# Two attention blocks with experts on one core: routers read raw rows, TensorE adds a residual, GpSimd a bias, and half of the second first-layer weights moves

## The reference

```
x = x + cross_attention_0(layernorm(x), ctx)     # 16 heads of 8, rotary, distance bias, gate
x = x + experts_0(layernorm(x))                  # 8 experts, top 2, 128 -> 512 -> 128, biases
x = x + cross_attention_1(layernorm(x), ctx)     # 16 heads of 8, biases, output W_O and b_O
x = x + experts_1(layernorm(x))                  # top 2 of 8, at most 321 pairs an expert, + its input
```

## Time and profile before

| | us |
|---|---|
| median of three executions | 300.12 |
| the profiled execution | 298.92 |
| its span in the profile | 297.2 |
| busy: TensorE / its weight loads | 219.6 / 178.3 |
| busy: VectorE / ScalarE / GpSimd | 154.0 / 113.4 / 143.8 |
| TensorE busy between 25 and 50, of 25 | 23.22 |
| TensorE busy between 75 and 90, of 15 | 6.38 |
| TensorE busy between 255 and 270, of 15 | 15.00 |

### The profile page before, as it was taken

How to read it: one execution, slowest core, us unless ns; L and a number is a source line. 1 busy time by engine, 2 the same in 40 slices (tenths; PEclk the granted TensorE clock), 3 DMA queues, 4 the chain that set the end, 5 groups by cost and what they waited for, 6 DMA issues and landing times.

```text
span 297.2 us, 4760 instructions
## 1 busy us (share of the span) xinstructions
PE 219.6 (74%) x1616; PEld 178.3 (60%) x1616; DVE 154.0 (52%) x509; ACT 113.4 (38%) x212; POOL 143.8 (48%) x201
## 2 busy tenths in 40 slices
PE   1779999998434589999904878998858069999900
PEld 1657776665323469999903666555445049999900
DVE  3985567766755524343204866587475313343206
ACT  1434667664020324444513248867300204433200
POOL 5652299433566414565645460320656713565730
PEclk9999999999555569999985999999555659999985
DMA  7999993000011270010157700000100153001125
GB/s 226 305 205 350 305 215 101 0 2 10 28 37 36 63 188 21 16 30 14 39 197 231 314 1 0 0 2 2 37 18 30 39 132 104 21 29 35 34 61 160
DMA packets 26960, 27.04 MB, mean 91 GB/s; under 512 B 3208, under 2 KB 23987, under 8 KB 26677
## 3 DMA queue, kind: packets, MB, share of 16 engines
q1 hardware_dynamic: 23776, 21.56, 26.5%
q0 software_dynamic: 2560, 4.08, 4.2%
q10 hardware_dynamic: 597, 1.06, 1.1%
HBM read 16.82 MB, written 10.79 MB: 93 GB/s over the span
## 4 chain that ended last, share of the span: by engine, by line
PE 51%; DVE 17%; DMA 9%; issue 7%; ACT 7%; POOL 7%; POOLq 1%; SPq 0%; DVEq 0%
PE ps L1491 14%; PE ps L1234 6%; ACT probT L681 5%; PE ps L1480 4%; PE ps L1481 4%; PE ps L1483 4%; POOL sent L532 3%; PE ps L1260 3%; DMA back<-probT,pairu 3%; DMA xe<-sent 2%; DVE stats L821 2%; PE ps L1240 2%; PE ps L1386 2%; DMA xe<-back 2%; PE ps L1206 2%
## 5 line engine op out<-in xcount | busy, mean ns | idle before, releaser
L579 POOL DMA_INDIRECT back<-probT,pairu x48 | 46.5, 968 | 31.8 <-issue 11.8
L1491 PE MATMUL ps<-w,hT 128*128 128x128 f32 (+1 forms) x384 | 49.5, 274 | 0.0
L1491 PEld LDWEIGHTS ps<-w,hT 128*128 128x128 f32 (+1 forms) x384 | 47.6, 182 | 0.1
L1186 PE MATMUL ps<-blank,identr 128*128 128x256 f32 x74 | 27.6, 533 | 22.4 <-DMA sent<-hidk,slotu 11.7
L532 POOL DMA_INDIRECT sent<-hidk,slotu x32 | 31.9, 996 | 22.0 <-DVE slotu L936 13.5
L681 ACT ACTIVATE probT<-ps 77x1024 f32<-77x1024 f32 x32 | 32.6, 1020 | 20.4 <-PE ps L1240 13.5
L1186 PEld LDWEIGHTS ps<-blank,identr 128*128 128x128 f32 x74 | 19.1, 273 | 26.8 <-issue 12.5
L842 DVE TENSOR_REDUCE peak<-ps 128x8 fp32r<-128x616 f32 x32 | 25.3, 792 | 17.2 <-PE ps L1206 16.9
L547 POOL TENSOR_TENSOR w1lo<-hT,w1hi 128x256 fp32r<-128x256 f32 x32 | 23.6, 742 | 18.5 <-ACT w1hi L659 16.7
L716 ACT ACTIVATE hT<-ps,col 128x384 f32<-128x384 f32 x32 | 18.1, 580 | 26.5 <-PE ps L1483 26.5
L1234 PE MATMUL ps<-qst,kst 100*78 100x256 f32 x128 | 25.0, 297 | 3.6 <-ACT probT L681 3.4
(11 more groups left out here) (165 smaller groups left out, 424.0 us busy)
## 6 DMA issues: line engine op xcount, KB each, us to landing
sent<-blank SPq DMA_DIRECT2D x16, 193.5 KB, 7.6
xe<-sent SPq DMA_DIRECT2D x16, 193.5 KB, 4.2
back<-blank SPq DMA_DIRECT2D x16, 128.0 KB, 4.5
hT<-w1b SPq DMA_DIRECT2D x4, 512.0 KB, 5.1
w<-w2b SPq DMA_DIRECT2D x1, 2048.0 KB, 13.3
hT<-w1d SPq DMA_DIRECT2D x4, 512.0 KB, 5.8
xe<-back SPq DMA_DIRECT2D x8, 256.0 KB, 3.6
w<-w2d SPq DMA_DIRECT2D x1, 2048.0 KB, 9.5
```

What stands on the lines that cost most here:

```text
L579: pool.indirect_dma_start(back[m], bass.IndirectOffsetOnAxis(ap=pairu[0:n, e, c:c + 1], axis=0), ye[0:n, e, c, :], None, bounds_check=NPAI ...
L1186: pe.matmul(ps[:, bank, 0:GQ], ident, blank[:, 0:2, 0:D], start=True, stop=True)
L1491: last = pe.matmul(ps[0:n, 6 + k % 2, c * P:(c + 1) * P], hT[:, e % 2, f, c * P:c * P + n], w2[:, e, f, :], start=(f == 0), stop=(f == FC ...
```

## The change

The routers' weights are centred once (TensorE multiplies them by the identity less 1/128), so that logits come from the rows themselves; the factor of the layernorm is put on the logits in `choose` (block 0) or on the difference of the two best (block 1). `turn` therefore transposes `xres`. In block 0 `lead` writes the gate's bias and, by a product with the identity, the residual into PSUM ahead of `project`, and `projected` goes. In block 1 GpSimd adds the output bias to the rows (`shifted`), and `residual` is one addition. Two pieces of the second first-layer weights go to `hid` and `hidb`, loaded when the experts have begun; the other two are loaded behind the gather. All steps get new places, now fractions of turns and one for each group; `due` sorts by them, and a turn of TensorE and ScalarE has several points at which steps are taken.

```diff
-WARM_TAIL = [{}, {20: 2, 21: 1, 23: 2, 24: 1}]
...
+PE_STEPS = [dict(lead=(7.73, 9.2, 13.8, 17.9),
+                 project=(7.83, 11.3, 15.73, 18.47),
+                 turn=(11.5, 15.76, 18.97, 19),
+                 logits=(12.86, 17.6, 19, 19.2),
+                 ranks=(14.64, 17.7, 19.03, 19.4),
+                 next_context=(14.2,),
+                 next_parts=(19.63,),
+                 next_keys=(19.66,)),
+            dict(project=(7.44, 12.97, 18.07, 18.13),
+                 turn=(9.4, 14.8, 18.31, 18.31),
+                 logits=(10.41, 16, 18.34, 18.34),
+                 ranks=(14.38, 18.1, 18.44, 19.33))]
+DVE_STEPS = [dict(taken=(7.5, 11.8, 15.27, 16.6),
+                 attended=(8.53, 12.33, 15.3, 17.1),
+                 residual=(10.07, 14.57, 17.6, 18.3),
+                 stats=(11.1, 14.7, 17.63, 18.7),
+                 hidden=(13.1, 15.9, 18.87, 20.03),
+                 choose=(14.7, 17.6, 18.83, 19.2),
+                 slots=(16.6, 17.8, 18.84, 19.4),
+                 next_context=(18.06,),
+                 next_parts=(20.63,),
+                 next_keys=(20.7,)),
+            dict(taken=(7.76, 11.6, 14.77, 17.1),
+                 attended=(9.34, 12.6, 15.3, 17.2),
+                 residual=(9.43, 14.57, 17.13, 17.6),
+                 stats=(10.2, 14.6, 17.17, 18.13),
+                 hidden=(10.63, 15.5, 20.43, 21),
+                 choose=(14.1, 17, 17.73, 20.53),
+                 slots=(15, 17.43, 19.9, 21))]
+ACT_STEPS = [dict(tanh=(8.47, 12.13, 17.4, 17.54),
+                 copies=(11.8, 17.13, 20.67, 20.7),
+                 turned=(12.43, 17, 17.57, 17.9),
+                 high=(0.17, 0.47, 3.56, 7.5, 7.93, 8.47, 10.94, 13.28)),
+            dict(copies=(14.44, 16.03, 19.22, 19.72),
+                 turned=(10.38, 15.01, 17.16, 18.19),
+                 high=(-1, -0.97, -0.94, -0.67, -0.64, 0.03, 6.66, 7.7))]
+POOL_STEPS = [dict(deviation=(18.07, 18.1, 19.87, 19.93),
+                 send=(18.1, 19.9, 19.93, 20.47),
+                 low=(3.22, 3.73, 3.76, 20.57)),
+            dict(deviation=(11.43, 11.43, 18.67, 19.1),
+                 shifted=(0, 0, 1.96, 2.09),
+                 residual=(11.46, 21, 21, 21),
+                 send=(16, 19.03, 20.16, 20.43),
+                 low=(-2, -1, 0.03, 4.59))]
...
+def due(steps, first, last):
+
+    return [(name, GROUPS - len(places) + g if len(places) < GROUPS else g)
+            for at, name, g, places in sorted((at, name, g, places) for name, places in steps.items()
+                                              for g, at in enumerate(places)) if first <= at < last]
...
+        early = [t[:].rearrange("p t d -> p (t d)").rearrange("p (e f) -> p e f", f=FF) for t in (hid, hidb)]
+
+        def first_raw(m, k):
+
+            if m == 0:
+                return raw[:, k % RAWS]
+            return early[k] if k < len(early) else raw[:, k - len(early)]
...
-                    sp.wait_ge(s_down[0], SC * E)
-                    sp.wait_ge(s_past, 1)
-                    for k in range(RAWS):
+                    sp.wait_ge(s_xres[0], GROUPS)
+                    sp.wait_ge(s_xT[0], PIECE)
+                    for k in range(len(early)):
                         first_weights(1, k)
...
+                    sp.wait_ge(s_past, 1)
+                    for k in range(len(early), PIECES):
+                        first_weights(1, k)
                     sp.dma_start(w2[:], w2d.rearrange("p (e c d) -> p e c d", e=E, c=FC)).then_inc(s_w2[1], 16)
-                    for k in range(RAWS, PIECES):
-                        first_weights(1, k)
...
+            def shifted(g):
+
+                pool.wait_ge(s_sum[0], GT * (g + 1))
+                bo = row[:, R_BO:R_BO + D].unsqueeze(1).broadcast_to([P, GT, D])
+                pool.tensor_tensor(base[:, of_group(g), :], xres[:, of_group(g), :], bo, ALU.add).then_inc(s_xb, 1)
...
-            low_weights(1, 0)
+            for name, k in due(POOL_STEPS[1], -9, 0):
+                low_weights(1, k)
             for g in range(GROUPS):
                 deviations(of_group(g))
...
+                if m == 1 and e == 0:
+                    act.wait_ge(s_past, 1)
...
 
                     dve.wait_ge(s_tanh, g + 1)
+                    if g == 0:
+                        dve.wait_ge(s_hbase, 2 * B)
+                    dve.scalar_tensor_tensor(out=ytok[:, s, :], in0=norm[:, s, :], scalar=1.0,
+                                             in1=ps[:, BY, :].rearrange("p (t n d) -> p t n d", t=GT, n=2)[:, :, 0],
+                                             op0=ALU.add, op1=ALU.mult).then_inc(s_yread, 1)
                     dve.wait_ge(s_yread, g + 1)
...
+                    dve.wait_ge(s_xb, g + 1)
+                    dve.tensor_tensor(xres[:, s, :], ps[:, BY, 0:GQ].rearrange("p (t d) -> p t d", t=GT), base[:, s, :],
+                                      ALU.add).then_inc(s_xres[1], 1)
+
+            def stats_of(m, g):
+
+                dve.wait_ge(s_xres[m], g + 1)
+                variances(xres[:, rows_of(g), :], GT, GT * g)
...
+                deviation = 1 + 2 * B + (GROUPS * 2 * m) + g + 1
                 if m == 0:
-                    bg = gbias[:].unsqueeze(1).broadcast_to([P, GT, E])
-                    link(dve.scalar_tensor_tensor(out=logit[:, s, :], in0=lp, scalar=GATE_DIV, in1=bg,
-                                                  op0=ALU.mult, op1=ALU.add))
-                else:
-                    link(dve.tensor_copy(logit[:, s, :], lp))
-                for t in range(GT * g, GT * g + GT):
-                    last = dve.max(top[:, t, :], logit[:, t, :])
+                    dve.wait_ge(s_rstd, deviation)
+                    for k in range(GT):
+                        t = GT * g + k
+                        last = dve.scalar_tensor_tensor(out=logit[:, t, :], in0=lp[:, k, :], scalar=rstd[:, t:t + 1],
+                                                        in1=gbias[:], op0=ALU.mult, op1=ALU.add)
...
+                if m == 1:
+                    dve.wait_ge(s_rstd, deviation)
+                    dve.tensor_tensor(wdif[:, s], wdif[:, s], rstd[:, s], ALU.mult).then_inc(s_dif[1], 1)
...
+            def lead(a, g):
+
+                if g == 0:
+                    pe.wait_ge(s_gate, 1)
+                    pe.wait_ge(s_hbase, 2 * B)
+                else:
+                    pe.wait_ge(s_yread, g)
+                    pe.wait_ge(s_tanh, g)
+                for k in range(GT):
+                    pe.matmul(ps[:, BY, k * GQ:(k + 1) * GQ], gateo, gater, start=(k == 0), stop=False,
+                              skip_group_check=True)
+                    pe.matmul(ps[:, BY, k * GQ:k * GQ + D], ident, hidb[:, GT * g + k, :], start=False, stop=False,
...
-                pe.wait_ge(s_hid[m], g + 1)
+                pe.wait_ge(s_xres[m], g + 1)
...
-                transposed(route_bank(g), lambda k: hidk[:, GT * g + k, 0, 0:D], GT).then_inc(s_hTp[m], 1)
+                transposed(route_bank(g), lambda k: xres[:, GT * g + k, :], GT).then_inc(s_hTp[m], 1)
...
+                    pe.wait_ge(s_slot[0], GROUPS)
+                    pe.wait_ge(s_most, 1)
...
+                pe.wait_ge(s_iset, 9)
+                pe.matmul(ps[:, BR, 2 * D:2 * D + 2 * E], centre, router[:].rearrange("p m e -> p (m e)"),
+                          start=True, stop=True)
...
+                    turn_steps(u, u + 0.2)
                     if u < UNITS:
                         shifted_scores(a, u)
+                    turn_steps(u + 0.2, u + 0.4)
                     query_steps(a, u + 2)
                     if u + 2 < UNITS:
                         maxima(a, u + 2)
                     if u + 3 < UNITS:
                         scores(a, u + 3)
+                    turn_steps(u + 0.4, u + 0.6)
                     if AHEAD <= u < UNITS + AHEAD:
                         attend(a, u - AHEAD)
-                    if u >= UNITS + AHEAD:
-                        warm_up(WARM_TAIL[a].get(u, 0), 1)
-                    for name, g in due(PE_STEPS[a], u):
-                        steps[name](a, g)
+                    turn_steps(u + 0.6, u + 1)
```

More of the change, by code:

```diff
@@ L79 @@
-ACT_STEPS = [dict(tanh3=4, tanh=5, copies=8, turned=8),
-             dict(copies=9, turned=7)]
-POOL_STEPS = [dict(deviation=9, residual=12, send=14),
-              dict(deviation=5, residual=7, send=10)]
+PE_STEPS = [dict(lead=(7.73, 9.2, 13.8, 17.9),
[10 more added lines that the diff above has]
+                 ranks=(14.38, 18.1, 18.44, 19.33))]
@@ L1135, in _ @@
             attention(0, 0)
-            for u in range(UNITS + max(DVE_STEPS[0].values())):
+            for u in range(last_turn(DVE_STEPS[0])):
+                for name, g in due(DVE_STEPS[0], u, u + 0.5):
+                    steps[name](0, g)
                 attention(0, u + 1)
                 query_steps(0, u)
-                for name, g in due(DVE_STEPS[0], u):
+                for name, g in due(DVE_STEPS[0], u + 0.5, u + 1):
```

(16 more changed lines are left out.)

158 lines of the change are left out of this document (70 added, 88 removed).

## The result

The changed kernel took 289.53 us (median of four, 288.74 to 291.52), the kernel before 301.36 beside it: ratio 0.964, 95% interval 0.955 to 0.974, faster. Six executions on another chip gave 292.2 against 300.45, ratio 0.974 (0.969 to 0.979). The ratios leave out executions that took over 1.5% longer than the fastest of the same kernel; the medians take in all. The forecast was 287.5, range 284.5 to 295. The profiled execution took 289.45 us, its span is 287.7 (before 297.2).

A forecast was written before the change was run, and what follows sets the result against it. Chains of waits at half clock, in two routing tails and the first block's returning rows, were taken as the bound. Sum: 298.92 + 0.5 - 2.7 - 3.4 - 5.8 = 287.5 us, range 284.5 to 295.

The forecast's parts named there:

- First attention: First block's attention loop: costs 0.5 us, between 0 and 1.8, with residual matmuls and moved steps on TensorE.
- First tail: Routing behind the first attention: last send at 96.55 instead of 99.62; gain 2.7 us, between 0 and 3.8.
- The experts: Both expert loops: untouched, no gain or cost forecast.
- Behind the first experts: Return of rows: no loads queued when the last scatter is issued, 5.44 becomes 2.03; gain 3.4 us, at least 2.4.
- Second attention and tail: Second block's attention and routing: last exponential at 209.0, last send at 232.2 instead of 237.97; gain 5.8 us.
- The subtraction is blocked: First tail: VectorE's products hold GpSimd's last subtraction, warm-up up to 2.9 us later, no tail gain; 290.3 us, chance 0.10.
- The low clock comes sooner: Second tail: clock falls before the last attention unit leaves, gain 3.5 instead of 5.8; 289.8 us, chance 0.18.
- The sends stay apart: Both tails: each removed wait is replaced by another, only the scatter gains; 296.0 us, chance 0.12.
- The loop loses the clock: Second attention: new waits drop TensorE to 1.2 GHz, 1.4 us a unit; slower, 310 us, chance 0.05.
- More: Both tails run without a gap on GpSimd, gains 3.8 + 3.4 + 7; 284.7 us, chance 0.08.

The follow-up runs named there:

- The old places: Changed kernel with the first block's steps back at their places before the change; four executions took 293.7, 287.94, 293.27 and 294.48 us.
- the rows first: Changed kernel with VectorE writing group 2's normalized rows ahead of its slot numbers in the first tail; 290.07 us, ratio 0.968.
- all five together: Changed kernel plus moved last and second subtractions (bias additions too), group 2's rows ahead of slots, key products on GpSimd, filling matmuls in second attention; 285.76 us, 0.950.
- the last subtraction moved: Changed kernel with the last subtraction of the first expert weights moved from behind the last send to between deviations 0 and 1; 289.69 us, ratio 0.960.
- the early loads alone: Kernel before with only two of four second first-layer weight pieces loaded under the first experts, the others behind the gather; ratio 0.992, medians 298.88 against 298.17.

## Why the prediction was right, point by point

The time came out 2 us above the forecast and well in the range, but the parts gave less than the sum: at their marks in the profiled executions they make 8.1 of the 11.4 us forecast, and 1.2 us came from the experts, for which the sum had nothing. That part is luck.

**First attention** (+0.5): the last exponential came 0.4 us later, but the last unit left TensorE at 74.05; forecast 74.04. The old places show the reason given: with them the logits stand ahead of the last unit again (74.94 to 75.48), with 0.8 us of the new step before that, and the unit leaves at 76.12.

**First tail** (-2.7): 1.2 us at the rows of expert 0. The last send left at 98.06 instead of 96.55, by two things. Send 2 started at 88.21, not 87.3, because the walk left out that ScalarE copies normalized rows which VectorE wrote behind the slots; with the rows first it started at 87.69. One DMA was held 0.8 us by VectorE's key product. The subtraction, 3.16 us as forecast, then held the warm-up, which the sum had priced at 0.4 us (103.55 against 103.14); without it the rows came 1.4 us sooner. With the collisions gone the last send left at 96.72, 0.2 from the 96.55 that the sum of GpSimd's steps gave: its idea was right.

**The experts** (nothing): 0.64 and 0.55 us less in the first and second stage. In the first, TensorE's granted clock was full 1.2 us behind the start of the rows (105.07), in the kernel before 3.4 us (106.27), both worked out from the mean clock of the window in which it rose (windows in the form given above; before, as changed, all five together):

```profile
109.00:110.00 1.00, 1.00 (x5) 1.00 (x5) 0.48 (x1) 0.58 (x1) 0.19 (x1) 0.65 1.09 309
```

```profile
106.00:107.00 1.00, 0.82 (x5) 0.45 (x3) 0.94 (x2) 0.00 (x0) 0.00 (x0) 0.89 1.11 313
```

```profile
106.00:107.00 1.00, 1.00 (x5) 1.00 (x4) 0.32 (x1) 0.58 (x1) 0.27 (x2) 0.56 1.15 272
```

In the kernel before, TensorE stood 1.28 us between the warm-up and the rows; as changed, the warm-up ran up to them. With all five changes the rows start at 103.11 and the clock is full 3.8 us later; from the rows to the last scatter it is 45.35 us (44.53 as changed, 45.17 before). What decides when the clock rises is not shown: with the last subtraction moved the warm-up ran up to the rows too, and the clock was full 3.1 us behind their start.

**Behind the first experts** (-3.4): mis-sized, 1.86. The scatter fell to 2.23 us, as said (-3.2). But the gather behind it rose from 3.00 to 3.68 (+0.7), which the sum left at its old length, and the first combining operation from 0.62 to 1.43 (+0.8). "GpSimd now subtracts two pieces ahead of the deviations ... so nothing" is the step that failed: the pieces were indeed done before the first deviation, but VectorE's combining ran beside them. The prediction looked for who waits for GpSimd and not for who works beside it, though it had named that collision a stage earlier. Why the gather is longer stays open: it was 3.45 with the early loads alone and 3.5 to 4.1 in the other runs that have them, and the two loads queued behind it are issued only from 154.87 on, 3.0 us after its start.

**Second attention and tail** (-5.8): 5.08 at the last send. The last exponential gained 2.7 (2.45 forecast), the last attention matmuls 4.75 (6.1), and the fifteen us from send 1 to the last (15.3; 15.8 forecast) were unbroken. That is with the clock at half from the last exponential on. In the five runs whose loop ended at the full clock the last send lay 52.2 us behind the first exponential, a gain of 6.8: for the case it was made for, the term was 1.0 too small.

**The rivals.** *The subtraction is blocked* came in another form: the subtraction took 3.16 us, but GpSimd's DMA was held beside VectorE's product, and VectorE's combining beside GpSimd's subtraction. *The low clock comes sooner* was true of the trace after: the clock fell 29.8 us behind the first exponential, as before, while the loop's last matmuls were still to come. The measured 289.5 is thus nearer to this rival's 289.8 than to the forecast, but not by its sum: the fall cost 1.6 us (3.64 against 2.07) instead of 2.3, the sends behind it were 0.5 shorter, and the tail gave 5.08 instead of 3.5; that the two numbers meet is chance, since the terms ahead of the tail fell short. *The sends stay apart* is what the old places of block 0 showed. *The loop loses the clock* didn't happen: the clock was full inside the first loop, and inside the second until the last exponential. (The sum of *More*, 284.7, leaves out the 0.5 of the first attention.)

## What to carry to other kernels

When work is moved on GpSimd, look at what VectorE does in the same microseconds, also where neither waits for the other: three such meetings took about 0.8 us each here. Another place or engine for the work undid two of them and a wait on a semaphore the third, each read from the marks of one trace. When a stage ends earlier, ask which clock it finds: rows that came 2.0 to 2.2 us sooner to TensorE made the last scatter only 1.1 to 1.4 us earlier. Where transfers are moved from one place in a chain, price scatter and gather together, 8.44 us here against 5.9.

## What the runs showed of the hardware

An indirect DMA that GpSimd issues took 0.97 us by itself, about 1.07 as the first of a send, and 1.46 to 2.15 where VectorE's product of two tiles in SBUF had begun before it (nine runs); 0.97 with the product gone (two runs). A DMA that was under way when the product began was not held: 0.97 in the kernel before, from 99.62 on, with the product from 100.01 on. The Trainium skill, "SBUF — State Buffer", section "Who interferes with whom", infers that such a product doesn't hold GpSimd's DMA issue, because that needs the write interface; here it did, and the measurement decides. That the issue reads its offsets from SBUF would fit the page's rule on GpSimd's reads; no run here separates that.

VectorE's `tensor_scalar` with one tile in SBUF, 128x128, took 0.57 us for two and 1.42 beside GpSimd's addition, which had started 0.06 us earlier and took 0.7 as ever. The same section counts it among the operations that can exclude GpSimd; the rows agree, and here VectorE was the one held.

The granted clock was not the same in each execution of the same instructions. At the first stacking of queries behind the last norm, eight matmuls took 1.19 us in the one run and 2.02 in the other (chain of waits, as changed and with the rows of group 2 first):

```profile
168.30 1.19 PE ps L1468 x8
```

```profile
168.37 2.02 PE ps L1468 x8
```

With half clock there, the way from the last scatter to the first exponential took 27.2 to 27.7 us (three runs), with the full one 24.3 to 25.9 (eight runs with early loads). This and the end of the loop, some 1.6 us each, would make up the 3 us by which executions differ; only one execution of each kernel has a trace, so that is an estimate. The Trainium skill, "TensorE: Matmul & The Clock Gate", Part 1, section "What's actually happening", calls the change of the clock "run-variable"; the traces agree.
